# An expert layer's up projection in three blocks of 112, 112 and 128 weight columns in place of four of 88

## What is computed

```
buf = jnp.zeros((E * C, H), x.dtype).at[slot].set(x[tok]).reshape(E, C, H)   # E = 64, C = 96, H = 256
g = jnp.einsum('ech,emh->ecm', buf, Wg)                                      # M = 176
u = jnp.einsum('ech,emh->ecm', buf, Wu)
out = jnp.einsum('ecm,ehm->ech', jax.nn.silu(g) * u, Wd).reshape(E * C, H)
yk = out[slot].reshape(T, K, H)
y = jnp.sum(yk * topk_w[..., None].astype(yk.dtype), axis=1)
```

## Time and profile before

| | |
|---|---|
| median of 3 runs | 1264.48 us (1261.58 to 1265.62) |
| span of the profiled execution | 1275.3 us |
| expert loop in the profile, first turn to last scatter issued | 1023.3 to 1221.9 us |
| PE busy over the span | 1182.9 us (93%) |
| DVE, ACT, POOL busy over the span | 911.6 us (71%), 865.0 us (68%), 664.7 us (52%) |
| DMA queues q1 (from SP and ACT) and q0 (from POOL), share of 16 engines | 59.7% and 5.1% |

### The profile page before, as it was taken

The page is one execution under the profiler, slowest core; times in us unless marked ns, Lnnn a source line. Parts: engine busy times, 40 slices in busy tenths (PEclk is TensorE's granted clock), DMA queues, the critical chain, the costliest instruction groups (busy, mean ns, idle before and its releaser), DMA issues.

```text
span 1275.3 us, 25192 instructions
## 1 busy us (share of the span) xinstructions
PE 1182.9 (93%) x7600; PEld 836.2 (66%) x7600; DVE 911.6 (71%) x2651; ACT 865.0 (68%) x2316; POOL 664.7 (52%) x746
## 2 busy tenths in 40 slices
PE   3899999999999999999999999999879798989985
PEld 1466666766666676676667666677535477868863
DVE  4887688799789889979988987887757232223336
ACT  3999779878878887887887788788625232323413
POOL 4564334336654655654664565466562523444557
PEclk9999999999999999999999999999989899999998
DMA  7686577867976665565566457456428379898676
GB/s 270 160 213 143 113 131 151 168 151 170 197 174 140 118 123 102 105 123 104 101 108 109 88 97 141 73 100 106 83 58 249 112 207 247 219 234 217 144 197 215
DMA packets 394759, 190.01 MB, mean 149 GB/s; under 512 B 317521, under 2 KB 373303, under 8 KB 394625
## 3 DMA queue, kind: packets, MB, share of 16 engines
q1 hardware_dynamic: 375040, 173.53, 59.7%
q0 software_dynamic: 16416, 11.70, 5.1%
q10 hardware_dynamic: 3168, 3.15, 0.7%
HBM read 75.32 MB, written 64.69 MB: 110 GB/s over the span
## 4 chain that ended last, share of the span: by engine, by line
PE 64%; DMA 11%; DVE 10%; issue 7%; ACT 6%; another core or an unknown queue 1%; SPq 1%; POOL 1%; ACTq 0%; DVEq 0%; POOLq 0%
PE bank L1144 15%; PE bank L1173 14%; PE bank L1188 11%; DMA Y<-W,wix 9%; PE bank L1159 7%; PE bank L1205 7%; PE bank L1237 3%; PE bank L1312 2%; PE bank L1325 2%; PE bank L1355 1%; DVE nm L1581 1%; PE bank L1271 1%; ACT P L1414 1%; DVE PH L1574 1%; DMA X<-in_x 1%
## 5 line engine op out<-in xcount | busy, mean ns | idle before, releaser
L1414 ACT ACTIVATE P<-bank,nm 128x256 f32<-128x256 f32 x512 | 237.9, 471 | 107.3 <-DVE nm L1581 97.1
L1144 PE MATMUL bank<-RB,W 128*128 128x512 f16 x1076 | 275.1, 381 | 5.3 <-DVE W L812 3.9
L1173 PE MATMUL bank<-RB 128*128 128x256 f32 x1024 | 244.6, 382 | 10.2 <-issue 6.9
L1074 POOL TENSOR_SCALAR P<-P,rr 128x256 f32<-128x256 f32 x256 | 121.1, 482 | 252.5 <-DVE rr L1563 244.2
L823 POOL DMA_INDIRECT BUF<-RT,ix x192 | 201.6, 1050 | 72.8 <-issue 37.6
L1173 PEld LDWEIGHTS bank<-RB 128*128 128x128 f32 x1024 | 185.7, 191 | 34.9 <-ACT RB L1385 6.6
L1144 PEld LDWEIGHTS bank<-RB,W 128*128 128x128 f16 x1076 | 105.2, 98 | 123.4 <-issue 8.8
L1581 DVE TENSOR_REDUCE nm<-bank 128x2 f32<-128x512 f32 x256 | 174.2, 681 | 11.0 <-PE bank L1173 8.8
L1205 PE MATMUL bank<-W,O 128*128 128x256 f16 x1060 | 158.8, 275 | 5.2 <-DVE O L1587 5.2
L1095 POOL DMA_INDIRECT Y<-W,wix x64 | 90.9, 1421 | 117.8 <-ACT W L1492 67.5
L1079 POOL TENSOR_TENSOR PH<-P,PH 128x512 f16<-128x512 f32 x86 | 101.2, 1176 | 87.3 <-ACT PH L1430 86.3
(11 more groups left out here) (224 smaller groups left out, 1995.4 us busy)
## 6 DMA issues: line engine op xcount, KB each, us to landing
RB<-in_ewT SPq DMA_DIRECT2D x24, 352.0 KB
BUF<-zrow SPq DMA_DIRECT2D x24, 321.0 KB, 3.3
W<-BUF SPq DMA_DIRECT2D x64, 120.4 KB
HT<-in_ewT SPq DMA_DIRECT2D x18, 352.0 KB
HT<-in_wc SPq DMA_DIRECT2D x24, 256.0 KB, 4.2
HT<-in_ws SPq DMA_DIRECT2D x24, 256.0 KB, 4.7
Y<-zrow SPq DMA_DIRECT2D x20, 256.0 KB
RB<-in_ewd SPq DMA_DIRECT2D x24, 176.0 KB
```

Source lines behind the costliest of these rows:

```text
L1074: r = eng.tensor_scalar(p, p, rr[:, w % 4, t:t + 1], SP_, ALU.mult, ALU.mult)
L1144: r = eng.matmul(bk_[:, :], W[:, m, a, c * 2048 + h * 128:c * 2048 + (h + 1) * 128], XT[:, bp % 2, b, c, :], start=(k == 0), stop=(k == n ...
L1173: r = eng.matmul(bS[u % 2][:, t * 256:(t + 1) * 256], QK[:, i % 2, 0, q * 256 + t * 128:q * 256 + (t + 1) * 128], QK[:, i % 2, 1, q * 256: ...
L1414: r = eng.activation(P[:, u % 2, t * 256:(t + 1) * 256], bS[u % 2][:, t * 256:(t + 1) * 256], ACT.Exp, bias=nm0[:, u % 4, t:t + 1], accum_ ...
```

## The change

The 176 hidden columns are cut as 112 + 64. The gate's first 112 and the value's first 112 are a block each, straight from `EG` (L1315 of the changed kernel). The 64 last columns of gate and value stand together as a third block of 128 columns. They do not lie side by side in `EG`, so DVE copies them into a tile `EC` (128 partitions by 2 x 2 x 64 elements, two buffers): a new function `e_cols`, called between `e_rows(e)` and `e_act(e-1)`. It waits for the weights of e and for `e_up` of e-2; `e_up` waits for it before its last two matmuls. So PE has 6 matmuls in place of 8 for an expert. Silu takes 112 partitions by 192 elements; the product is in two instructions, 112 x 96 and 64 x 96, since the third block has its gate in partitions 0 to 63 and its value in 64 to 127. The down projection still has two matmuls, with 112 and 64 rows in place of 88 and 88. For that, `ED` is loaded by three DMAs of 1 KB rows (88, 24 and 64 rows) in place of one of 88 rows of 2 KB.

```diff
-                eng.dma_start(ED[b][0:88, :], ewd[e]).then_inc(s_ew[b], 16)
+                eng.dma_start(ED[b][0:88, 0:256], ewd[e][:, 0:256]).then_inc(s_ew[b], 16)
+                eng.dma_start(ED[b][88:NA, 0:256], ewd[e][0:NA - 88, 256:512]).then_inc(s_ew[b], 16)
+                eng.dma_start(ED[b][0:64, 256:512], ewd[e][NA - 88:88, 256:512]).then_inc(s_ew[b], 16)
...
                 for m in range(2):
-                    for j in range(2):
-                        for c in range(2):
-                            o = (m * 2 + c) * 176 + j * 88
-                            r = eng.matmul(bS[e % 2][0:88, (m * 2 + j) * CAP:(m * 2 + j + 1) * CAP],
-                                           EG[b][:, o:o + 88], BT[:, e % 2, c * CAP:(c + 1) * CAP],
-                                           start=(c == 0), stop=(c == 1))
+                    for c in range(2):
+                        o = (m * 2 + c) * 176
+                        eng.matmul(bS[e % 2][0:NA, m * CAP:(m + 1) * CAP], EG[b][:, o:o + NA],
+                                   BT[:, e % 2, c * CAP:(c + 1) * CAP], start=(c == 0), stop=(c == 1))
+                eng.wait_ge(s["ec"], e + 1)
+                for c in range(2):
+                    r = eng.matmul(bS[e % 2][:, 2 * CAP:3 * CAP], EC[:, e % 2, c, :, :].rearrange("p m n -> p (m n)"),
+                                   BT[:, e % 2, c * CAP:(c + 1) * CAP], start=(c == 0), stop=(c == 1))
                 r.then_inc(s["eg"], 1)
...
-                for j in range(2):
-                    r = eng.matmul(bP1[0:CAP, 0:256], ac2[0:88, e % 2, j, :],
-                                   ED[b][0:88, j * 256:(j + 1) * 256], start=(j == 0), stop=(j == 1))
+                for j, n in enumerate((NA, 64)):
+                    r = eng.matmul(bP1[0:CAP, 0:256], ac2[0:n, e % 2, j, :],
+                                   ED[b][0:n, j * 256:(j + 1) * 256], start=(j == 0), stop=(j == 1))
...
-                eng.tensor_tensor(ac2[0:88, e % 2, :, :].rearrange("p j n -> p (j n)"), bS[e % 2][0:88, 192:384],
-                                  sl2[0:88, e % 2, :], ALU.mult).then_inc(s["eac"], 1)
+                eng.tensor_tensor(ac2[0:NA, e % 2, 0, :], bS[e % 2][0:NA, CAP:2 * CAP],
+                                  sl2[0:NA, e % 2, 0:CAP], ALU.mult).then_inc(s["eac"], 1)
+                eng.tensor_tensor(ac2[0:64, e % 2, 1, :], bS[e % 2][64:128, 2 * CAP:3 * CAP],
+                                  sl2[0:64, e % 2, CAP:2 * CAP], ALU.mult).then_inc(s["eac"], 1)
+
+            def e_cols(e):
+                b = e % NRING
+                eng.wait_ge(s_ew[b], 64 * (e // NRING + 1))
+                if e >= 2:
+                    eng.wait_ge(s["eg"], e - 1)
+                eng.tensor_copy(EC[:, e % 2, :, :, :],
+                                EG[b].rearrange("p (m c n) -> p c m n", m=2, c=2)[:, :, :, NA:176]
+                                ).then_inc(s["ec"], 1)
...
                     e_rows(e)
+                    e_cols(e)
```

16 lines of the change are left out of this document (10 added, 6 removed).

## The result

The changed kernel takes 1270.09 us (median of 4 runs, 1268.66 to 1271.34) where the kernel before takes 1263.82 us (4 runs). The ratio is 1.0059, with a 95% interval of 1.0041 to 1.0077: slower by 0.6%. The forecast was 1264 us and no change that can be told. The time lies inside the forecast's range, which reaches from 1256 to over 1271 us, but the kernel is slower by more than its interval.

The account below looks back on a forecast made before the run. The prediction took the chain of scatters, each waiting for the landing two before, as the bound, with PE hidden. Only an earlier start counted, -0.4 us, with DVE, SP and DMA at 0: 1264.48 - 0.4, 1264 us; range 1256 to over 1271.

Parts of the forecast that it names:

- What bounds the kernel: Expert loop: each scatter waits for the landing two before, 6.04 us for two experts; PE's work is hidden.
- the split over engines is not in the trace: Loop's DMA loads: the argument given against the rival that relieving the fullest DMA engine gains 5 us.
- Up: PE's up projection: 1.20 us in place of 1.33, loads 95 and 109 ns apart, saving 8.5 us in 64 experts, hidden.
- two matmuls whose columns and loads don't change: nothing: PE's down projection: it keeps two matmuls, so its time was forecast to change by nothing.
- four issues took some 1.6 us of 3.0; six take 2.35 ... 0 us: SP's load issues for an expert: two more cost 0.78 us but fit in the expert's time, effect 0 us.
- DVE: Copy (0.41 us) and extra product add 0.57 us an expert; effect 0 us, 5.2 us if uncovered.
- The held-up POOL (rival at 0.13): Scatters: DVE's copy holds POOL, up to 0.41 us a link; half the time gives 1271 us; chance 0.13.
- DMA: Down weight loads in smaller packets and three DMAs: 0 us, between +3 and -5 us.
- the relief of the fullest engines: Down weight loads: three DMAs give the fullest DMA engine 14 KB in place of 16, -5 us, 1259 us; chance 0.13.
- Smaller losses together: Loop: longer landings by DMA packets and DVE's 5.2 us uncovered at places, 1269 us; chance 0.09.
- PE is the bound after all: Expert loop: PE sets the time, so its 8.5 us saving gives 1256 us; chance 0.10.
- scatters 0.8 us behind their `e_out`: Loop's scatters: a sign that the forecast is wrong and PE was last.

Follow-up runs that it names:

- before_less_pe: Kernel before with the last of eight up matmuls left out, old down weight loads kept: 1260.39 us, ratio 0.9988 to the kernel before.
- no_copy: Changed kernel with down weights in two loads, second down matmul over 96 rows, third block laid side by side by the host, no DVE copy: 1254.11 us, ratio 0.9953.
- no_copy_more_pe: no_copy with the first matmul of each up projection done twice, transfers unchanged: 1254.88 us, ratio 0.9942 to the kernel before.
- down_88_64: Kernel before with the second down matmul over 64 rows in place of 88, loads unchanged: 1288.52 us, ratio 1.0027 to the kernel before.
- no_copy_b: no_copy run again on another chip: 1274.76 us, ratio 0.9938 to the kernel before.
- after_two_loads_k96_b: Changed kernel with down weights in two loads (112 and 64 rows) and second down matmul over 96 rows, copy kept: 1275.43 us, ratio 0.9942 to the kernel before.
- after_k96: Changed kernel with the second down matmul over 96 rows in place of 64, added activations zero: 1265.44 us, ratio 1.0030 to the kernel before.
- split_loads: Kernel before with each expert's down weights in three loads (88, 24, 64 rows of 1 KB) in place of one: 1293.02 us, ratio 1.0054.
- copy_alone: Kernel before with only the new DVE copy and the wait for it before the last two up matmuls: 1283.58 us, ratio 0.9988.
- before_two_loads: Kernel before with down weights in two loads of 88 rows of 1 KB in place of one of 2 KB: 1276.34 us, ratio 1.0002.
- after_two_loads: Changed kernel with down weights in two loads (112 and 64 rows) in place of three: 1258.88 us, ratio 0.9977 to the kernel before.
- after_again: Changed kernel, unchanged, run again on another chip: 1270.07 us, ratio 1.0077 to the kernel before.
- before_96_rows: Kernel before with each down weight load over 96 rows of 2 KB in place of 88, 8 rows repeated: 1277.81 us, ratio 0.9992.

## Why the prediction was right or wrong

**What bounds the kernel.** Right as far as it went. In the kernel before PE's work is hidden: 10 us taken from it (before_less_pe) changed nothing that can be told, and 0.2 us an expert added to no_copy (no_copy_more_pe) didn't either. The cover has an end: 0.32 us an expert added (down_88_64) came through as 3.5 us. The chain of scatters was the right place to look, but its links are made of landings, and what sets those is probably the throughput of the fullest DMA engines: the links are 5.72 to 5.80 us for two experts in no_copy, no_copy_b, no_copy_more_pe and after_two_loads_k96_b, and 5.99 to 6.07 in the four profiles of the kernel before. The prediction called 0.89 a sign of queueing and went on. Its "the split over engines is not in the trace" holds for the rows; the semaphore events tell how many engines a load has.

**Up.** Nearly right: 1.23 us against 1.20. The matmul records are 98 and 112 ns apart in the median, not 95 and 109, so PE saves 0.10 us an expert, 6.4 us in 64, not 0.13 and 8.5. That such a saving is hidden is right (before_less_pe).

**Down: "two matmuls whose columns and loads don't change: nothing".** Wrong, and the first failed step. The number of rows changed from 88 to 64, and I took rows for free, since no row of the trace showed a switch. It costs 0.27 us in down and 0.05 in the turn: PE's round is 2.58 us, not 1.20 + 0.86 + 0.17 = 2.23. down_88_64 shows it alone at +0.27%, and after_k96 takes 4.6 us back. Why a load of 64 rows next to 88 or 112 stands still, no run shows.

**SP: "four issues took some 1.6 us of 3.0; six take 2.35 ... 0 us".** Wrong, the largest term. The prices of the earlier trace rows are those of issues in a queue with pauses. Back to back the six take 3.28 us, and an expert of the loaded stage took no more than that; the 3.0 us that the prediction compared with is the mean of the whole loop. split_loads shows it alone at +0.54%. One issue fewer gives 11.2 us, which includes a more even split. The prediction had named who is queued behind, the token rows, and that they are needed six experts later. It didn't ask what happens when the queue is never empty: any lead is used up.

**DVE.** 0 us was right, and the copy is 0.28 us. The estimate of 0.29 us by the Trainium skill, VectorE: DVE Perf Modes, The perf-mode tier table, was the better one; my row of 0.41 was an arithmetic operation with a scalar, not a copy. The held-up POOL (rival at 0.13) didn't show: its scatter keeps its median of 1.41 us in the changed kernel, and 1.42 in the mean of copy_alone.

**DMA.** I took 0 between +3 and -5 us. Kernels with loads of 112 and 64 rows are 7 to 9 us faster, which the relief of the fullest engines would explain. With 88, 24 and 64 rows, as in the change, it can't be read apart, because SP has the loop. 1 KB packets cost nothing (before_two_loads).

**The sum as measured.** The parts of the change, each alone in the kernel before: loads in three +0.54% (split_loads), 64 rows +0.27% (down_88_64), the copy -0.12% with an interval through no change (copy_alone). A shorter up gave -0.12%, also with an interval through no change (before_less_pe). The first three make +0.69%, where the change measured +0.59 and +0.77. Each of these has an interval of some 0.2 to 0.3% either way. Taken back from the changed kernel, 64 rows are 0.35 (after_two_loads to after_two_loads_k96_b) to 0.47% (after_again to after_k96), and the third load is 1.0% (after_again less after_two_loads). The 1.0% includes what 88 and 24 rows may lose of the even split; these two weren't parted.

**The rivals.** "Smaller losses together" gave 1269 us, which is nearly the time, but by luck: the losses are others than it named. No rival was SP. "PE is the bound after all" was rightly small for the kernel before; in the changed kernel PE did become last, slower by its gaps and its waits. That the time lies inside the range is luck too, since the range was drawn for other causes. Two of the prediction's signs came true: scatters 0.8 us behind their `e_out`, and links of (1214.71 - 1017.23) / 31 = 6.37 us, which it gave as the sign of a held POOL. POOL wasn't held, so a longer link alone doesn't name its cause.

**What stays open.** The loop of the changed kernel is 210.7 and 209.7 us in its two profiles, that of the kernel before 196.9 to 201.5 us in four, so 8 to 14 us longer, and the timed difference is 6 to 10 us. No profile of the unchanged kernel has the early start; before_less_pe on one had a loop of 194.4 us, so part of the difference is likely the chip's. How the gain of the loads of 112 and 64 rows comes about is argued, and why before_96_rows has so little of it isn't settled. What makes the chips differ ahead of the loop wasn't looked for.

## What to carry to other kernels

Price an issuing queue by its fill, not by single rows: add up the issues of a round at their back-to-back price and compare with the round's length in the same stage, since beyond it every lead is used up. When a mean DMA share stands at 0.9 and landings are what is waited for, look at how the rows of each load divide among 16 engines before anything on PE. And an edit whose saving lies on an engine that isn't last can still be worth it for what it does to the loads: here the version with loads of 112 and 64 rows is 0.6% faster, with or without PE's saving.
